# Dummy products on TensorE ahead of a group norm's variance and between the steps of a token router

## The chip, the cores and the metric

The kernel runs on one NeuronCore of a Trainium2 chip. The metric is the device time of one execution in microseconds (us). Five engines work side by side, each on its own list of instructions: TensorE (PE in the profile, its weight loads PEld), VectorE (DVE), ScalarE (ACT), GpSimd (POOL) and SyncE (SP), which issues the transfers. They wait for each other through semaphores that the kernel sets by hand. TensorE's clock has two levels, 1.2 and 2.4 GHz; the profile shows the granted clock as a share of the upper one, so 0.50 is 1.2 GHz and 1.00 is 2.4 GHz.

## The reference

Two transformer-like layers with adaptive layer norms, each an attention-like part and a feed-forward part. The input has 2048 tokens of 128 features. The change touches the first layer only, in two places. Cut to these:

```python
# layer 0, attention part (16 heads of 8 features, scan over 2048 tokens)
S = dt[..., None] * S + kv ; o = einsum('bhk,bhkv->bhv', rt, S_old + u * kv)
mean = jnp.mean(o, axis=-1, keepdims=True)          # group norm over each head
var = jnp.var(o, axis=-1, keepdims=True)
o = (o - mean) * jax.lax.rsqrt(var + EPS_GN) * gn_w + gn_b
x = x + (o * g).reshape(B, T, D) @ Wo
...
# layer 0, feed-forward part: each token goes to one of 8 experts, 128 places each
routes = softmax(x @ w_switch + b_switch).argmax(-1)
oh = (routes[:, None] == jnp.arange(E)[None, :]).astype(jnp.int32)
pos = (jnp.cumsum(oh, axis=0) * oh).sum(-1) - 1
keep = pos < capacity
slot = jnp.where(keep, routes * capacity + pos, E * capacity)
buf = zeros.at[slot].set(x)                          # dispatch
```

The second layer (a Mamba-like scan over 16 states and a mixture of 16 experts plus a shared one) follows and takes the time from about 240 us to the end.

## The kernel before, in words

Features or head values lie on the 128 partitions, the 2048 tokens along the free dimension, in 4 chunks of 512. One chunk is one PSUM bank of TensorE's output. `sequences()` (L166) lists, by engine, every step in the order in which that engine does it; `upto(step, i)` turns a step into the semaphore value to wait for, `done(step, i)` into the increment at its end. Each engine works its list strictly in that order, so an instruction whose data are ready still stands behind the one before it.

**The group norm.** After the scan, each chunk i goes through: `gn_centred` on TensorE (L728, subtracts the head's mean by a matrix product), `gn_sq` on ScalarE (L1148, a square; the helper's line also serves other squares), `gn_var` on TensorE (L733, the mean of squares, into PSUM bank `VAR_BANK[i]`), then on ScalarE `gn_ln` (L1248), `gn_rs` (L1250) and `gn_rs2` (L1252). ScalarE takes chunk i to its end before it squares chunk i+1. So its list is a chain that goes to TensorE and back once a chunk. VectorE scales and normalizes (L1670, L1676, L1678), GpSimd multiplies by the gate (L2008), TensorE multiplies by `Wo` (L739, L743). TensorE's order around the change comes from `TAIL_PE` (L154): at turn 33 of the loop at L753 it does four `reduce` products (L776), `gn_centred(1)`, `gn_var(0)`, `gn_var(1)`, `gn_centred(2)`; then come the last `reduce` products, `gn_var(2)`, `gn_centred(3)` and so on (L780 to L794). Chunk 0's `gn_centred` was done two turns earlier, and its square is made while TensorE does the reduces.

**The router.** On TensorE: `varD` (L812), 16 small products for the logits (`router`, L840, recorded as two each), 8 transposes of the layer's input (`h_turn`, L845), a wait for VectorE's one-hot matrix (`r_oh`), the products `prefix` and `totals` (L850, L851), 8 more transposes, a wait for VectorE's kept slots (`r_kept`), a transpose of the slots (`slot_turn`, L855) and then 16 times `dispatch(t)` (L864), four products of 512 columns each. VectorE (L1736 for all its router steps) goes from the logits to `r_oh`, then `r_shift`, `r_base`, a rounding remainder (L1754), and, once `totals` is there, `r_cum` to `r_kept`. Then it makes `onehot(t)` (L1784) in two buffers: `onehot(t)` waits for `dispatch(t - 2)`, `dispatch(t)` for `onehot(t)`.

The constants that the change uses are `EYEB` (128x128, bf16) and `sel` (96 x 32 x 128, bf16). They are loaded at the start (L631, L632) and counted by `wc_loaded`.

Of the kernel before, what the change touches and what calls it, by code (L numbers as in the profile page):

```python
# [152 lines left out]
VAR_BANK = (2, 0, 3, 1)  # L153
# [212 lines left out]
def build(nc, X_in, vec_in, core_in, cst_in, wA_in, wmod_in, cstB_in, wB1_in, wB2_in, wC_in, sel_in, eyeb_in, wD_in, out):  # L366
# [17 lines left out]
    with ctx:  # L384
        def sb(name, shape, dt=f32):
            return ctx.enter_context(nc.sbuf_tensor(name, shape, dt))

        def sem(name):
            return ctx.enter_context(nc.semaphore(name))

        vec_loaded, core_loaded, wmod_loaded, cst_loaded, wa_loaded, cstb_loaded, wb_loaded, wc_loaded, out_stored = map(
            sem, ["vec_loaded", "core_loaded", "wmod_loaded", "cst_loaded", "wa_loaded", "cstb_loaded", "wb_loaded", "wc_loaded", "out_stored"])
# [11 lines left out]
        def upto(step, i=0):  # L404

            engine, n = count[step, i]
            return finished[engine], n

        def done(step, i=0):

            engine, n = count[step, i]
            assert order[engine].pop(0) == (step, i), (step, i)
            return finished[engine], 1
# [5 lines left out]
        def column(step, q):  # L419

            return upto(step.format(ORDER[q % DK]), q // DK)
# [15 lines left out]
        sel = sb("sel", [96, 2 * NS, P], bf16)  # L437
        BC = sb("bc", [96, T], bf16)
        EYEB = sb("eyeb", [P, P], bf16)
# [20 lines left out]
        def CORE_(name):  # L460
            a, w = core_at[name]
            return core[:, a:a + w]

        def C(name, part=slice(None)):
            a, w = cst_at[name]
            return cst[part, a:a + w]
# [5 lines left out]
        def CB_(name):  # L472
            a, w = cb_at[name]
            return cstB[:, a:a + w]
# [121 lines left out]
        def ch(buf, i, off=0):  # L596

            return buf[:, i * N + off:(i + 1) * N + off]

        def half(h, i, rows=P):  # L600

            return ps[0:rows, (4 * h + i) * N:(4 * h + i + 1) * N]

        def bank(b, lo=0, hi=P):
            return ps[lo:hi, b * N:(b + 1) * N]
# [72 lines left out]
        def _(pe):  # L678
            mm = nc.tensor.matmul
# [36 lines left out]
            def gate_and_bonus(i):  # L716
# [5 lines left out]
                pe.wait_ge(*(upto("bonus", i - 1) if i else upto("w_exp", 1)))  # L722
                mm(bank(1), C("head_sum"), ch(M2, i), start=True, stop=True).then_inc(*done("head_ruk", i))

            def gn_centred(i):
                pe.wait_ge(*upto("o", i))
                pe.wait_ge(*column("scan{}", NR - NCH + i))
                mm(half(1, i), C("gn_centre"), ch(O, i), start=True, stop=True).then_inc(*done("gn_centred", i))  # L728

            def gn_var(i):  # L730
                pe.wait_ge(*upto("gn_sq", i))
                pe.wait_ge(*(column("scan{}", (2 * DK - 1) if i == 0 else NR - 1) if i % 2 == 0 else upto("o", LAST - 1 + i // 2)))
                mm(bank(VAR_BANK[i]), C("gn_mean"), ch(T1, i), start=True, stop=True).then_inc(*done("gn_var", i))  # L733
# [11 lines left out]
            def ms_c(i):  # L745
                pe.wait_ge(*upto("sqC", i))
                pe.wait_ge(*upto("gn_norm", i))
                mm(bank(VAR_BANK[i]), CORE_("mean"), ch(T2, i), start=True, stop=True).then_inc(*done("msC", i))

            tail = {"gn_centred": gn_centred, "gn_var": gn_var}  # L750
            lora_b(0)
            pe.wait_ge(*upto("spread_r"))
            for q in range(NR + LAG_R - 1):  # L753
                i, v = q // DK, ORDER[q % DK]
# [12 lines left out]
                if q >= LAG_R and (q - LAG_R) % 4 == 0:  # L767

                    pe.wait_ge(*column("prod{}", q - LAG_R + 3))
                    for r in range(q - LAG_R, q - LAG_R + 4):  # L770
                        i, v = r // DK, ORDER[r % DK]
# [5 lines left out]
                for name, i in TAIL_PE.get(q, ()):  # L777
                    tail[name](i)

            gn_var(2)  # L780
            gn_centred(3)
            wo_b(0)
            gn_var(3)
            wo(0)
            wo_b(1)
# [58 lines left out]
            def h_turn(t):  # L844
                nc.tensor.transpose(ps[:, 4 * N + t * P:4 * N + (t + 1) * P], HB[:, t * P:(t + 1) * P], CORE_("eye")).then_inc(*done("h_turn", t))  # L845

            for t in range(NT // 2):
                h_turn(t)
            pe.wait_ge(*upto("r_oh"))
            mm(bank(1)[:, 0:P], CB_("tri"), small(3), start=True, stop=True).then_inc(*done("prefix"))  # L850
            mm(bank(2)[:, 0:P].rearrange("p (e t) -> p e t", e=E0), CB_("ones"), small3(3).rearrange("p t e -> p e t"), start=True, stop=True).then_inc(*done("totals"))  # L851
            for t in range(NT // 2, NT):
                h_turn(t)
            pe.wait_ge(*upto("r_kept"))
            nc.tensor.transpose(bank(1, 0, NT)[:, 2 * P:3 * P], tiny(9), CORE_("eye")).then_inc(*done("slot_turn"))  # L855
            for t in range(NT):
                if t == SCALE_AT:
                    pe.wait_ge(*upto("r_scale"))
                    nc.tensor.transpose(bank(2, 0, NT)[:, 2 * P:3 * P], tiny(4), CORE_("eye")).then_inc(*done("scale_turn"))
                pe.wait_ge(*upto("onehot", t))  # L860
                pe.wait_ge(*upto("h_turned_lo", t // 4))
                for part in range(2):
                    for j in range(2):
                        last = mm(bank(3 * j), HT[:, part, t * P:(t + 1) * P], OH1[:, t % 2, j * N:(j + 1) * N],  # L864
                                  start=(t == 0 and part == 0), stop=(t == NT - 1 and part == 1))
                last.then_inc(*done("dispatch", t))
# [242 lines left out]
            for q in range(NQ):  # L1109
                i, n = divmod(q, NS)  # L1110
# [1127 lines left out]
```

## Time and profile before

| | us |
|---|---|
| three runs | 658.53, 660.23, 660.22 (median 660.22) |
| the profiled execution, its own time | 658.89 |
| its span, first to last instruction | 657.1 |
| TensorE busy | 564.2 (86%) |
| VectorE busy | 530.9 (81%) |
| ScalarE busy | 392.1 (60%) |
| GpSimd busy | 394.3 (60%) |
| mean granted clock of TensorE | 0.953 |

The three runs and the profiled one lie at two levels 1.7 us apart. What lies outside the span is 658.89 - 657.1 = 1.8 us. Busy shares are means over stages that differ: the two places of the change lie at 103 to 118 us and at 160 to 191 us of the span. In a timeline row a group of like instructions is merged: the first number is its start, the second the time that it covers, xN how many there are, and the bracket says how long the engine stood idle before it and what released it. A 128x512 product on fp32 data is recorded as two.

### The profile page before, as it was taken

How to read it: one execution, taken by the hardware profiler on the slowest of the kernel's cores; microseconds unless marked ns; L12 is line 12 of the kernel's file. 1: busy time of each engine (PE TensorE's matmuls, PEld its weight loads, DVE VectorE, ACT ScalarE, POOL GpSimd, SP SyncE). 2: the span in 40 equal slices, each digit the busy share in tenths (PEclk: the TensorE clock that was granted, in tenths of full speed). 3: DMA queues.
4: the chain of work that ended last, by engine and by line, in shares of the span. 5: the costliest groups of instructions: out<-in, count | busy, mean ns of one | idle time of the engine just before them, and what ended most of it. 6: DMA issues, size and time to landing. Idle time of an engine off the chain costs nothing.

```text
span 657.1 us, 6791 instructions
## 1 busy us (share of the span) xinstructions
PE 564.2 (86%) x1896; PEld 316.2 (48%) x1896; DVE 530.9 (81%) x727; ACT 392.1 (60%) x672; POOL 394.3 (60%) x345
## 2 busy tenths in 40 slices
PE   6698668899899868688888768878879999999997
PEld 3233222366678523233333323323336768888885
DVE  1979997656779676699999999999998857666664
ACT  5675324686123497777966756766565475555553
POOL 0035886651000201389999999999976546566665
PEclk9798878999699999699999899999999999999999
DMA  8100000700110001000001000000103334434330
GB/s 309 37 1 0 0 1 9 332 1 1 65 65 0 1 0 48 1 0 0 0 5 44 24 25 24 24 14 7 43 0 104 107 105 123 129 111 145 109 102 17
DMA packets 14598, 35.13 MB, mean 53 GB/s; under 512 B 1952, under 2 KB 2240, under 8 KB 13952
## 3 DMA queue, kind: packets, MB, share of 16 engines
q1 hardware_dynamic: 14560, 34.69, 16.5%
q8 instruction: 16, 0.26, 0.2%
q14 instruction: 22, 0.18, 0.1%
HBM read 33.48 MB, written 1.20 MB: 53 GB/s over the span
## 4 chain that ended last, share of the span: by engine, by line
DVE 19%; PE 14%; issue 13%; POOL 10%; ACT 3%; POOLq 0%; DVEq 0%; ACTq 0%
DVE arena L1928 13%; POOL h_parts L2144 9%; PE ps L1079 7%; DVE arena L1903 5%; PE ps L1014 4%; POOL arena L2008 1%; PE ps L1117 1%; PE ps L942 1%; PE ps L1051 0%; ACT ps L1488 0%; ACT arena L1477 0%; PE ps L1026 0%; ACT L1435 0%; ACT arena L1437 0%; DVE arena L1912 0%
## 5 line engine op out<-in xcount | busy, mean ns | idle before, releaser
L2008 POOL TENSOR_TENSOR arena<-arena 128x512 f32<-128x512 f32 x184 | 226.0, 1256 | 24.0 <-DVE arena L1928 19.1
L1928 DVE TENSOR_TENSOR_SCAN arena<-ps,carry,arena 128x512 f32<-128x512 f32 x128 | 156.5, 1265 | 0.0
L1014 PE MATMUL ps<-arena,core 128*128 128x512 f32 x256 | 126.7, 613 | 1.3 <-POOL arena L2008 0.8
L1488 ACT ACTIVATE ps<-arena,abase 128x512 f32<-128x512 f32 x128 | 88.0, 691 | 63.9 <-DVE arena L1928 63.0
L2144 POOL TENSOR_TENSOR h_parts<-arena,h_parts 128x512 fp32r<-128x512 f32 x68 | 87.8, 1291 | 62.1 <-ACT h_parts L1528 61.1
L1079 PE MATMUL ps<-x_parts,w_hi 128*128 128x512 f32 x272 | 100.4, 408 | 0.4 <-DVE arena L2001 0.4
L1903 DVE TENSOR_TENSOR arena<-ps,arena 128x1024 f32<-128x1024 f32 x64 | 76.9, 1202 | 5.8 <-PE ps L1117 5.8
L1996 DVE TENSOR_TENSOR ps<-ps,arena 128x512 f32<-128x512 f32 x64 | 44.6, 698 | 43.0 <-PE ps L1079 36.7
L1117 PE MATMUL ps<-bc,sel 96*128 96x512 bf16 x128 | 44.2, 393 | 40.7 <-ACT arena L1477 23.8
L1536 ACT ACTIVATE arena<-ps 128x512 f32<-128x512 f32 x68 | 40.6, 599 | 61.3 <-PE ps L1079 60.2
L1014 PEld LDWEIGHTS ps<-arena,core 128*128 128x128 f32 x256 | 48.5, 194 | 42.2 <-issue 22.4
L1079 PEld LDWEIGHTS ps<-x_parts,w_hi 128*128 128x128 f32 x272 | 51.2, 188 | 14.6 <-issue 1.4
L1117 PEld LDWEIGHTS ps<-bc,sel 96*128 96x128 bf16 x128 | 12.2, 98 | 92.6 <-ACT arena L1477 37.8
L1079 PE MATMUL ps<-x_parts,wD 128*128 128x512 f32 x136 | 54.0, 397 | 0.0
L1079 PE MATMUL ps<-h_parts,w_hi 128*128 128x512 f32 x136 | 53.4, 396 | 0.3 <-POOL h_parts L2144 0.3
L2059 POOL TENSOR_TENSOR x<-arena,x 128x512 f32<-128x512 f32 x4 | 5.3, 1320 | 71.6 <-DVE arena L1829 71.6
L2001 DVE TENSOR_TENSOR arena<-ps,arena 128x512 f32<-128x512 f32 x64 | 44.2, 691 | 2.2
L1528 ACT ACTIVATE h_parts<-arena 128x512 fp32r<-128x512 f32 x68 | 42.4, 623 | 4.8 <-DVE arena L2001 4.2
L1477 ACT ACTIVATE arena<-ps 128x512 f32<-128x512 f32 x64 | 37.3, 583 | 1.0 <-PE ps L1117 0.7
L761 PE MATMUL ps<-v_parts,spread_r 128*128 128x512 f32 x64 | 26.7, 521 | 11.9 <-DVE arena L1661 11.9
L2012 POOL TENSOR_TENSOR v_parts<-arena,v_parts 128x512 fp32r<-128x512 f32 x4 | 6.3, 1613 | 41.1 <-ACT v_parts L1202 41.1
L1661 DVE TENSOR_TENSOR_SCAN arena<-arena,ps 128x512 f32<-128x512 f32 x24 | 29.7, 1262 | 0.0
(256 smaller groups left out, 1003.4 us busy)
## 6 DMA issues: line engine op xcount, KB each, us to landing
arena<-weight_rows SPq DMA_DIRECT2D x64, 256.0 KB, 3.3
arena<-in_wB SPq DMA_DIRECT2D x2, 2048.0 KB, 12.6
arena<-in_wD SPq DMA_DIRECT2D x8, 384.0 KB, 3.1
arena<-in_cstB SPq DMA_DIRECT2D x1, 1368.0 KB, 5.9
wC<-in_wC SPq DMA_DIRECT2D x1, 1056.0 KB, 11.7
x<-in_x SPq DMA_DIRECT2D x4, 256.0 KB, 4.6
arena<-slot_rows SPq DMA_DIRECT2D x4, 256.0 KB, 3.6
arena<-scale_rows SPq DMA_DIRECT2D x4, 256.0 KB, 3.6
```

The lines of the kernel that those rows point to most:

```text
L1014: mm(bank(c + 2 * (i % 2)), CORE_("eye"), PRC[:, (2 * q + c) % PR_RING, :], start=False, stop=(n == NS - 1)).then_inc(*done(f"y{n}_{c}", i))
L1079: r = mm(out, w_parts[wp][:, k, :], x[xp], start=start and (wp, xp) == (0, 0), stop=stop and last)
L1117: mm(bank(b), sel[:, row, :], BC[:, i * N:(i + 1) * N], start=True, stop=True).then_inc(*done(f"{kind}{n}", i))
L1488: A(bank(6 + c), ch(DTG[:, c, :], i), ACT.Exp, scale=ABASE[:, c * NS + n:c * NS + n + 1]).then_inc(*done(f"dec{n}_{c}", i))
L1528: A(HWP[:, 0, q % 4, :], (HW if e < E1 else HH)[:, q % H_RING, :], ACT.Copy).then_inc(*done(f"h_hi{e}", i))
L1536: A(SG[:, q % 2, :], bank(4 + q % 2), ACT.Silu).then_inc(*done(f"silu{e}", i))
L1903: tt(DBU[:, a:a + DI, :], bank(4).unsqueeze(1).to_broadcast([P, DI, N]), DU[:, :, i * N:(i + 1) * N], ALU.mult).then_inc(*done(f"dbu{n}", i))
L1928: nc.vector.tensor_tensor_scan(ST[:, k % ST_RING, :], bank(6 + c), DBU[:, (2 * q + c) % DBU_RING, :], CARRY[:, k:k + 1], ALU.mult, ALU.add ...
L1996: tt(bank(6 + k) if e < E1 else HH[:, h, :], bank(6 + k), SG[:, k, :], ALU.mult).then_inc(*done(f"hh{e}", i))
L2001: tt(HW[:, h, :], bank(6 + k), ROW[r % W_SLOTS], ALU.mult).then_inc(*done(f"hw{e}", i))
L2008: mul = lambda o, a, b: nc.gpsimd.tensor_tensor(o, a, b, ALU.mult)
L2144: nc.gpsimd.tensor_tensor(HWP[:, 1, q % 4, :], (HW if e < E1 else HH)[:, q % H_RING, :], HWP[:, 0, q % 4, :].bitcast(f32), ALU.subtract).t ...
```

## The change

A helper `keep_busy(b, n)` issues n products of the constants `EYEB` and `sel` (96 rows, 128 columns of weights, 512 moving columns, bf16) into PSUM bank b. Nothing reads them and they increment no semaphore. Ten stand ahead of the waits of `gn_var(0)`, with a wait for the constants' loads; five ahead of the wait for `r_oh`, eight ahead of the wait for `r_kept`, and two between `slot_turn` and the first `dispatch`.

```diff
@@ -722,12 +722,20 @@
+            def keep_busy(b, n):
+
+                for _ in range(n):
+                    mm(bank(b), EYEB[0:96, :], sel[:, 0:4, :], start=True, stop=True)
+
...
             def gn_var(i):
+                if i == 0:
+                    pe.wait_ge(wc_loaded, 48)
+                    keep_busy(VAR_BANK[0], 10)
                 pe.wait_ge(*upto("gn_sq", i))
...
@@ -846,13 +854,16 @@
             for t in range(NT // 2):
                 h_turn(t)
+            keep_busy(3, 5)
             pe.wait_ge(*upto("r_oh"))
             mm(bank(1)[:, 0:P], CB_("tri"), small(3), ...).then_inc(*done("prefix"))
             mm(bank(2)[:, 0:P]..., CB_("ones"), ...).then_inc(*done("totals"))
             for t in range(NT // 2, NT):
                 h_turn(t)
+            keep_busy(3, 8)
             pe.wait_ge(*upto("r_kept"))
             nc.tensor.transpose(bank(1, 0, NT)[:, 2 * P:3 * P], tiny(9), CORE_("eye")).then_inc(*done("slot_turn"))
+            keep_busy(3, 2)
             for t in range(NT):
```

## Rows read from the trace of the kernel before

**Rows 1.** Windows: us, then each engine's busy time, granted clock (PEclk), DMA; group norm.

```profile
core 0: us, PE busy (x) PEld busy (x) DVE busy (x) ACT busy (x) POOL busy (x), PEclk, DMA share, GB/s
104.50:108.00 3.50, 1.15 (x3) 0.19 (x1) 2.63 (x4) 2.25 (x4) 3.50 (x4) 1.00 0.00 0
108.20:111.40 3.20, 3.16 (x4) 1.17 (x4) 0.92 (x2) 1.02 (x2) 1.27 (x2) 0.50 0.00 0
```

**Rows 2.** Windows, the router and the dispatch.

```profile
160.90:165.10 4.20, 3.81 (x33) 3.62 (x32) 2.44 (x4) 1.88 (x4) 0.00 (x0) 1.00 0.00 0
166.20:169.40 3.20, 2.07 (x9) 2.04 (x10) 2.72 (x9) 0.98 (x3) 0.00 (x0) 0.50 0.00 0
173.00:176.20 3.20, 3.20 (x9) 2.52 (x8) 1.70 (x3) 0.00 (x0) 0.00 (x0) 0.50 0.63 213
176.50:180.00 3.50, 3.25 (x14) 2.00 (x13) 3.26 (x8) 0.00 (x0) 0.00 (x0) 1.00 0.24 81
```

**Rows 3.** Timeline of TensorE, group norm: start, us, engine, line, op.

```profile
103.67 1.13 PE L728 MATMUL ps<-arena 128*128 128x512 f32 x2
104.63 1.02 PE L733 MATMUL ps<-arena 128*128 128x512 f32 x2
108.24 2.07 PE L733 MATMUL ps<-arena 128*128 128x512 f32 x2 [2.59 <-ACT arena L1148]
...
112.90 1.12 PE L733 MATMUL ps<-arena 128*128 128x512 f32 x2
```

**Rows 4.** Timeline of ScalarE, group norm.

```profile
102.78 0.60 ACT L1148 ACTIVATE arena<-ps 128x512 f32<-128x512 f32 x1 [0.46 <-PE ps L728]
105.69 0.69 ACT L1248 ACTIVATE arena<-ps,vec 128x512 f32<-128x512 f32 x1 [2.31 <-PE ps L733]
...
107.60 0.58 ACT L1148 ACTIVATE arena<-ps 128x512 f32<-128x512 f32 x1
110.35 0.69 ACT L1248 ACTIVATE arena<-ps,vec 128x512 f32<-128x512 f32 x1 [2.16 <-PE ps L733]
...
114.06 0.69 ACT L1248 ACTIVATE arena<-ps,vec 128x512 f32<-128x512 f32 x1 [1.22 <-PE ps L733]
```

**Rows 5.** Timeline of TensorE, two bf16 products in a row at full clock.

```profile
295.84 0.60 PE L1117 MATMUL ps<-bc,sel 96*128 96x512 bf16 x2
296.28 1.02 PE L1014 MATMUL ps<-arena,core 128*128 128x512 f32 x2
```

**Rows 6.** Timeline of TensorE, the router.

```profile
165.12 1.07 PE L845 MATMUL ps<-core,arena 128*128 128x128 f32 x8
167.33 0.79 PE L850 MATMUL ps<-arena 128*128 128x128 f32 x2 [1.14 <-DVE arena L1736]
...
168.39 1.89 PE L845 MATMUL ps<-core,arena 128*128 128x128 f32 x8
170.63 0.38 PE L855 MATMUL ps<-core,arena 128*16 128x128 f32 x1 [0.35 <-DVE arena L1736]
171.42 8.26 PE L864 MATMUL ps<-onehot,h_turned 128*128 128x512 f32 x24 [0.41 <-DVE onehot L1784]
```

**Rows 7.** Timeline of VectorE, the router and the dispatch.

```profile
168.68 0.42 DVE L1736 TENSOR_TENSOR_SCAN arena<-arena,ps 128x128 f32<-128x128 f32 x1 [0.27 <-PE ps L851]
...
170.61 1.42 DVE L1784 TENSOR_SCALAR onehot<-arena 128x1024 fp32r<-128x1024 f32 x2
...
173.53 0.75 DVE L1784 TENSOR_SCALAR onehot<-arena 128x1024 fp32r<-128x1024 f32 x1 [0.91 <-PE ps L864]
175.24 0.75 DVE L1784 TENSOR_SCALAR onehot<-arena 128x1024 fp32r<-128x1024 f32 x1 [0.95 <-PE ps L864]
...
186.43 0.75 DVE L1784 TENSOR_SCALAR onehot<-arena 128x1024 fp32r<-128x1024 f32 x1 [0.29 <-PE ps L864]
...
188.47 0.75 DVE L1784 TENSOR_SCALAR onehot<-arena 128x1024 fp32r<-128x1024 f32 x1 [0.31 <-PE ps L864]
```

**Rows 8.** Timeline, the end of the dispatch and ScalarE's copy that waits for it.

```profile
190.50 0.60 ACT L1320 ACTIVATE arena<-ps 128x512 f32<-128x512 f32 x1 [4.74 <-PE ps L864]
```

## The prediction

> **What bounds the kernel now.** I read the windows with the granted clock first, since the change adds work that nothing uses and can pay only through the clock of TensorE. The clock is at 2.4 GHz up to 108.0 us, at 1.2 GHz from 108.2 to 111.4 us [rows 1], and again at 1.2 GHz from 166.2 to 176.2 us [rows 2]. Both falls come behind little streaming on TensorE: 2.59 us of idleness before the second variance product [rows 3], and the logits' products from 160.9 to 165.1 us [rows 2], whose moving operand has 8 columns. Then I read the timelines around the two places. In the group norm the chain is ScalarE's: its logarithm of chunk 0 begins at 105.69 us, that of chunk 1 at 110.35, that of chunk 2 at 114.06 [rows 4], so a round takes 4.66 us with the variance product at half clock (2.07 us) and 3.71 us with it at full clock (1.12 us) [rows 3]. In the router the chain is VectorE's, with TensorE's `prefix` and `totals` in between, and from 171.42 us on it is the dispatch on TensorE and the one-hots on VectorE, which release each other [rows 6, 7]. All that follows hangs on the end of the dispatch at 190.50 us [rows 8].
>
> **The price of one dummy product.** Two bf16 products of the same size take from 295.84 to 296.28 us, so 0.22 us each at full clock [rows 5]. At half clock a product costs twice that: an fp32 variance product goes from 1.12 to 2.07 us [rows 3], and four dispatch products at half clock set a pace of 175.24 - 173.53 = 1.71 us, 0.43 each [rows 7]. I take 0.22 and 0.43 us.
>
> **Ten products ahead of gn_var(0).** The square that `gn_var(0)` waits for begins at 102.78 us and takes 0.60, so it is ready at 103.38 [rows 4], before `gn_centred(1)` begins at 103.67. `gn_var(0)` begins at 104.63, right behind the 1.13 us of `gn_centred(1)`, with no idle time in its row [rows 3]. There is no wait here to fill. The ten products go between the two and push `gn_var(0)` back by 10 x 0.22 = 2.2 us, and with it ScalarE's logarithm at 105.69, which had waited 2.31 us for just this product [rows 4]. The rest of the chain starts from there, so 2.2 us are on the path; the added wait for the loads is free, since they are over long before.
>
> What comes back is the half clock of `gn_var(1)`, at most 4.66 - 3.71 = 0.95 us. But the idle stretch of 2.59 us lies between `gn_var(0)` and `gn_var(1)` [rows 3], that is behind the new products, and it stays as long as it was: logarithm, exponential, square, square on ScalarE. The products only move it later. So the clock may fall all the same and catch `gn_centred(2)` or `gn_var(2)`. Bounds: 2.2 - 0.95 = 1.25 us where the fall is avoided, 2.2 + 0.95 = 3.15 us where a second product is caught as well. I take half of the 0.95 as won: **+1.7 us**.
>
> The Trainium skill (TensorE: Matmul & The Clock Gate, on why this matters for kernels) asks for a TensorE kept busy without gaps between bursts. By it the ten products would be a gain where they bridged a gap; the row shows none ahead of `gn_var(0)`, so the sum above goes by the row.
>
> **Five products ahead of r_oh.** TensorE is idle for 1.14 us before `prefix` at 167.33 [rows 6]. Five products last 1.1 us at full clock and 2.15 at half. The fall at 166.2 us follows from the logits' products before it, which the change leaves as they are, so I take half clock: `prefix`, `totals` and all of VectorE's steps behind them (`totals` releases the scan at 168.68 [rows 7]) come 2.15 - 1.14 = 1.0 us later. Bounds: 0 and 1.0.
>
> **Eight products ahead of r_kept and two behind slot_turn.** Before, the second transposes last from 168.39 to 170.28 us, then there are 0.35 us of idleness, the slots' transpose at 170.63, and the first dispatch at 171.42 [rows 6]. What decides is when the clock is back. From 108.2 us steady work brought it back after some 3.3 us [rows 1]. In the router it took until between 176.2 and 176.5 us, since there the work had holes until the dispatch began at 171.42 [rows 2, 6]. The dummy products close the holes, so from 166.2 us on TensorE is all but busy.
> - Clock back near 169.5 us: by then five products, `prefix` and `totals` are done; eight transposes at full clock 1.1 us (1.07 at 165.12 [rows 6]), eight products 1.8, `slot_turn` 0.3, two products 0.4: the dispatch begins near 173.1 us. At full clock two turns take 188.47 - 186.43 = 2.04 us [rows 7], so 1.02 to 1.07 each with VectorE's side work, 16 turns about 17.1: it ends at 190.2 against 190.5 [rows 8], -0.3 us.
> - Clock back near 172.9 us: transposes 1.9, most of the eight products at 0.43; the dispatch begins near 174.4 and ends at 191.5, +1.0 us.
> - Bounds: the clock never at half: dispatch from 171.5, all 16 turns at full clock, end at 188.6, -1.9 us. Clock back no sooner than before: 1.0 + 8 x 0.43 + 2 x 0.43 = 5.3 us less the idle 0.35 and 0.4 that they fill, so a start at 175.9, and an end near 193.0, +2.5 us.
>
> I take **+0.2 us**, between the first two and nearer to the first. The loads of the slots' rows and the scale's rows move with `slot_turn` and stay hidden by the experts' work; no queue but TensorE's has anything put ahead. PSUM banks 2 and 3 are free there, so nothing else waits for the dummies.
>
> **Sum.** 1.7 + 0.2 = +1.9 us. Against the profiled execution, 658.89, that makes 660.8. The median of the three runs, 660.22, is 1.3 above it; the four times of before lie at two levels and have a mean of 659.5, so I add the sum to that: **661.4 us**, 0.2% over the median. About 0.3% (2.0 us: 658.2 to 662.2) is what a measurement can tell from no change, and the forecast lies inside, near its upper end.
>
> **The rivals.**
> - *The routing's dummies run at half clock throughout (slower).* Eight products stand before a wait of 0.35 us; at half clock they are 3.4 us ahead of `slot_turn` and thereby of every dispatch. The point that decides is whether the clock is back before they begin. For it: nothing in the change touches the products that made it fall, and it stayed low through `prefix`, `totals` and transposes before [rows 2, 6]. Against it: the holes are closed. 659.5 + 1.7 + 2.5 = 663.7 us. Chance 0.27.
> - *The clock is held at both places.* 1.25 - 1.9 = -0.65 us, 658.9 us. For it: the group norm's clock was up for all of `gn_var(0)`. Against it: the logits. Chance 0.15. The Trainium skill's rule cited above, taken for the whole change, comes to this case.
> - *The ten products cost nothing.* That needs a wait ahead of `gn_var(0)` that the row of the trace hides, or slack in ScalarE's chain: then -0.95 - 1.9 = -2.85, 656.7 us. Against it: rows 3 and 4 show neither. Chance 0.08.
> - *The forecast.* Chance 0.50. Its own range is 659.9 to 662.9: group norm 1.25 to 2.2, router -0.3 to +1.0, and half a microsecond for the level on which the runs fall.
>
> **How the numbers follow.** Faster by over 0.3% (below 658.2): the third rival 0.08 and the lower part of the second 0.04, so 0.12. Slower by over 0.3% (above 662.2): the first rival 0.25, the upper part of the forecast 0.18, so 0.43. Within: 0.45. The range for 8 in 10 takes in the forecast, most of the first rival and most of the second: 658.7 to 663.9 us.
>
> **What would show it.** In the changed kernel's timeline ten rows of bf16 products between the second L728 and the first variance product, that product about 2.2 us later, and ScalarE's wait for it 4.5 instead of 2.3 us. The idle time between the first and the second variance product near 2.6 us again. In the windows, a half clock that still begins between 163 and 168 us but ends before 173. The first dispatch between 172.5 and 174.5 us, taken without the shift of the group norm, and one-hots at a pace of 1.0 us from the first. The forecast is wrong if the first variance product does not move, or if TensorE's idleness behind it is gone; wrong for the router if the granted clock there is 1.00 throughout, or 0.50 during most of the dispatch.

## The result and the profile after

The changed kernel takes 663.75 us (median of 6 runs, 662.0 to 664.63) against 659.94 us before (6 runs, 658.53 to 660.31): a ratio of 1.0061 with an interval of 1.0046 to 1.0075, slower by 3.8 us. The forecast was 661.4 us, a loss of 1.2 us against the median. The profiled execution took 663.61 us with a span of 661.7, so 4.6 us more than the 657.1 of before.

I followed the extra time along the kernel by putting the same instruction of both traces side by side:

| instruction | before, us | after, us | delay |
|---|---|---|---|
| logarithm of chunk 0 (L1248, after L1259) | 105.69 | 107.79 | +2.1 |
| logarithm of chunk 1 | 110.35 | 111.53 | +1.2 |
| logarithm of chunk 2 | 114.06 | 116.05 | +2.0 |
| logarithm of chunk 3 | 117.77 | 119.76 | +2.0 |
| first router step of VectorE | 165.37 | 168.14 | +2.8 |
| router's scan, released by `totals` | 168.68 | 172.95 | +4.3 |
| VectorE's copy at the end of the dispatch | 190.50 | 192.82 | +2.3 |
| `bc_r1` of the second layer, its last of four (L1837, after L1848) | 263.13 | 266.08 | +2.9 |
| last of the state's expansion (L1903) | 494.51 | 497.89 | +3.4 |
| first product of the last experts (L1996) | 502.05 | 506.76 | +4.7 |

So three parts make the 4.6 us: the group norm 2.0, the router 0.3, and 2.3 behind the dispatch, where no line of the kernel was changed.

**Group norm.** TensorE's timeline of the changed kernel, the rows that answer to [rows 3] (L728 is now the line of the dummies, L733 `gn_centred`, L741 `gn_var`, L784 the `reduce` products):

```profile
103.60 1.12 PE L733 MATMUL ps<-arena 128*128 128x512 f32 x2
104.57 2.32 PE L728 MATMUL ps<-sel,eyeb 96*128 96x512 bf16 x10
106.73 1.02 PE L741 MATMUL ps<-arena 128*128 128x512 f32 x2
110.33 1.16 PE L741 MATMUL ps<-arena 128*128 128x512 f32 x2 [2.59 <-ACT arena L1159]
111.30 1.91 PE L733 MATMUL ps<-arena 128*128 128x512 f32 x2
113.13 1.82 PE L784 MATMUL ps<-arena 128*32 128x512 f32 x8
```

The ten dummies fill 106.73 - 104.57 = 2.16 us and move the first variance product by the same amount (104.63 to 106.73 us). The idle time behind it is 2.59 us, to the hundredth what it was. ScalarE's wait for that product, 2.31 us in [rows 4], is longer by the dummies:

```profile
107.79 0.69 ACT L1259 ACTIVATE arena<-ps,vec 128x512 f32<-128x512 f32 x1 [4.47 <-PE ps L741]
...
111.53 0.69 ACT L1259 ACTIVATE arena<-ps,vec 128x512 f32<-128x512 f32 x1 [1.25 <-PE ps L741]
...
116.05 0.69 ACT L1259 ACTIVATE arena<-ps,vec 128x512 f32<-128x512 f32 x1 [2.02 <-PE ps L741]
```

The windows of the same stretch, columns as in [rows 1]:

```profile
104.50:107.70 3.20, 3.20 (x13) 1.26 (x11) 1.63 (x2) 0.00 (x0) 3.20 (x3) 1.00 0.00 0
107.80:111.20 3.40, 0.86 (x2) 0.49 (x3) 2.00 (x3) 2.42 (x4) 0.00 (x0) 1.00 0.00 0
111.40:114.60 3.20, 3.20 (x11) 0.43 (x9) 0.69 (x1) 2.43 (x4) 1.20 (x1) 0.50 0.00 0
```

The clock falls all the same, at 111.3 instead of 108.1 us. The second variance product is now at full clock (1.16 instead of 2.07 us), which wins back 0.9 us at chunk 1; but `gn_centred(2)` (1.91 us, before 1.71) and the `reduce` products (1.82 us, before 1.06) are caught, and at chunk 2 the delay is 2.0 us again.

**Router.** TensorE's timeline, the rows that answer to [rows 6] (L848 the logits, L853 transposes, L859 and L860 `prefix` and `totals`, L865 `slot_turn`, L875 `dispatch`):

```profile
166.16 1.88 PE L848 MATMUL ps<-arena 128*128 128x8 f32 x8 [0.18 <-DVE arena L1567]
167.89 1.95 PE L853 MATMUL ps<-core,arena 128*128 128x128 f32 x8
169.63 2.34 PE L728 MATMUL ps<-sel,eyeb 96*128 96x512 bf16 x5
171.76 0.64 PE L859 MATMUL ps<-arena 128*128 128x128 f32 x2
172.19 0.66 PE L860 MATMUL ps<-arena 128*128 128x128 f32 x2
172.67 1.06 PE L853 MATMUL ps<-core,arena 128*128 128x128 f32 x8
173.56 1.89 PE L728 MATMUL ps<-sel,eyeb 96*128 96x512 bf16 x8
175.29 0.27 PE L865 MATMUL ps<-core,arena 128*16 128x128 f32 x1
175.40 0.59 PE L728 MATMUL ps<-sel,eyeb 96*128 96x512 bf16 x2
175.69 6.25 PE L875 MATMUL ps<-onehot,h_turned 128*128 128x512 f32 x24
```

```profile
166.00:172.60 6.60, 6.44 (x25) 5.19 (x26) 2.90 (x10) 1.45 (x3) 0.00 (x0) 0.50 0.01 2
...
172.90:178.00 5.10, 5.10 (x28) 3.32 (x27) 4.62 (x11) 1.35 (x3) 0.00 (x0) 1.00 0.01 2
```

The clock fell at about the same time of the record as before (165.9), but the work is 2 us later, so the last logits and the first transposes are caught too (1.88 instead of 1.06 us, and 1.95 instead of 1.07). The five dummies take 2.13 us at half clock and hold `prefix` back; that is the +4.3 us at the scan. Then the clock is back after 6.8 instead of 10.2 us, the whole dispatch runs at full clock, and 2 us come back by its end. As much comes back in e1 below, without any of the router's dummies.

**Behind the dispatch.** Two stretches at half clock are new or longer. These are windows of the kernel before, at the entry to the last experts:

```profile
490.50:493.70 3.20, 3.20 (x8) 1.66 (x8) 3.20 (x4) 1.90 (x3) 3.20 (x4) 0.50 0.00 0
494.00:497.00 3.00, 3.00 (x13) 1.75 (x13) 2.64 (x4) 1.25 (x3) 1.88 (x3) 1.00 0.00 0
```

and of the changed one, at the same work:

```profile
493.70:497.00 3.30, 3.30 (x10) 1.97 (x9) 3.30 (x4) 1.90 (x3) 3.30 (x4) 0.50 0.00 0
497.10:500.30 3.20, 3.20 (x7) 1.61 (x7) 2.50 (x4) 1.29 (x2) 1.81 (x3) 0.50 0.00 0
```

TensorE is the bound there (fully busy), and four products that took 1.88 us at full clock take 3.05 (the first row is of before, the second of the changed kernel):

```profile
494.52 1.88 PE L1014 MATMUL ps<-arena,core 128*128 128x512 f32 x4
498.07 3.05 PE L1025 MATMUL ps<-arena,core 128*128 128x512 f32 x4
```

With their neighbours that makes +1.3 us between the last two lines of the table. The other is a stretch from 261.6 to 264.8 us. Before, the same work was at full clock:

```profile
258.30:265.00 6.70, 3.83 (x10) 1.78 (x11) 3.34 (x7) 6.56 (x10) 4.02 (x4) 1.00 0.35 117
```

In the changed kernel the delay is 2.0 us ahead of this stretch (0.4 us had come back near 248 us) and 3.0 us behind it:

```profile
261.60:264.80 3.20, 3.20 (x5) 1.13 (x5) 0.22 (x1) 2.93 (x4) 1.88 (x2) 0.50 0.61 229
265.00:268.20 3.20, 2.12 (x7) 0.95 (x6) 2.06 (x3) 2.67 (x5) 2.28 (x3) 1.00 0.00 0
268.40:278.40 10.00, 5.85 (x9) 2.24 (x10) 6.20 (x6) 8.13 (x13) 2.50 (x3) 0.50 0.00 1
```

### The profile page after: what moved, and what is told of

It is laid out like the page before. It is cut to its first block, busy times and chain, and to the rows that moved or that the text cites. A ratio compares the mean times of both kernels' runs of the same rounds, so it can differ in the third digit from the quotient of the medians.

```text
span 661.7 us, 6841 instructions
## 1 busy us (share of the span) xinstructions
PE 572.1 (86%) x1921; PEld 319.2 (48%) x1921; DVE 530.8 (80%) x727; ACT 392.2 (59%) x672; POOL 394.1 (60%) x345
## 4 chain that ended last, share of the span: by engine, by line
PE 16%; DVE 15%; issue 13%; POOL 13%; ACT 3%; POOLq 0%; DVEq 0%; ACTq 0%
DVE arena L1939 10%; POOL h_parts L2155 9%; PE ps L1090 7%; PE ps L1025 5%; DVE arena L1914 4%; POOL arena L2019 4%; PE ps L1128 1%; PE ps L953 1%; PE ps L1062 1%; ACT ps L1499 1%; ACT arena L1488 0%; PE ps L1016 0%; ACT L1446 0%; PE ps L1055 0%; PE ps L1037 0%
## 5 line engine op out<-in xcount | busy, mean ns | idle before, releaser
L1025 PE MATMUL ps<-arena,core 128*128 128x512 f32 x256 | 128.5, 622 | 1.1 <-POOL arena L2019 0.7
L953 PE MATMUL ps<-arena,wC 128*128 128x512 f32 (+1 forms) x48 | 27.7, 708 | 2.7 <-ACT arena L1388 2.7
```

The costliest lines, as they stand in the source:

```text
L1025: mm(bank(c + 2 * (i % 2)), CORE_("eye"), PRC[:, (2 * q + c) % PR_RING, :], start=False, stop=(n == NS - 1)).then_inc(*done(f"y{n}_{c}", i))
```

## The experiments

**Theory.** The group norm's dummies stand where TensorE did not wait and are paid in full; the router's are near neutral; the rest is not work of the dummies, but the delay, which moves the second layer against the moments at which the clock falls. **Rivals:** the router's dummies are the main cost; the dummies themselves cost something in the second layer; a part of them is hidden.

The 16 profiles differ by up to 2.6 us before 40 us already, whatever the kernel. Seven of them (e1, e4, e6, e8, e9, e12, e14) have a half-clock stretch that begins at 17 to 18 us, which the other nine lack, and they reach the group norm 1.2 us or more later than any of the nine. So every delay of the profiles in the table is counted from one and the same scan of VectorE ahead of the group norm (before: 104.37 us, the seven 106.0 to 106.4, the nine 103.8 to 104.8), against the profile of before. "Dispatch" is VectorE's copy at its end, "last" one of its last instructions (654 us). Each ratio is to the runs of before that were taken beside that kernel. The edits of e1, e2, e8, e10 and e12 are shown against the changed kernel, those of e3, e4, e7 and e9 against the kernel before, where the helper `keep_busy` is added and not shown.

| profile of | chunk 0's logarithm | chunk 3's | dispatch | last | median of the runs | ratio to before, interval |
|---|---|---|---|---|---|---|
| the change | +2.2 | +2.1 | +2.4 | +4.7 | 663.75 | 1.0061, 1.0046 to 1.0075 |
| e1, group norm's ten alone | +2.2 | +2.1 | +0.9 | +0.4 | 659.81 | 1.0011, 0.9984 to 1.0037 |
| e2, router's alone | 0.0 | 0.0 | -1.2 | +0.4 | 660.31 | 1.0012, 0.9992 to 1.0033 |
| e3, nine in the wait | 0.0 | -0.9 | -2.2 | -3.3 | 658.42 | 0.9979, 0.9951 to 1.0006 |
| e4, ten copies on ScalarE | +1.0 | +1.8 | +0.5 | -0.3 | 660.67 | 1.0008, 0.9989 to 1.0026 |
| e5, the change again | +2.2 | +2.0 | +2.4 | +4.6 | 663.91 | 1.0056, 1.0037 to 1.0074 |
| e6, before again | 0.0 | 0.0 | 0.0 | +1.6 | 660.48 | 1.0011, 0.9991 to 1.0031 |
| e7, twenty at the group norm | +4.3 | +3.4 | +3.3 | +3.2 | 663.02 | 1.0047, 1.0032 to 1.0062 |
| e8, nine in the wait and the router's | 0.0 | -0.9 | -0.7 | -0.2 | 659.28 | 0.9998, 0.9984 to 1.0012 |
| e9, eleven behind the dispatch | 0.0 | 0.0 | 0.0, then +2.3 | +4.6 | 665.28 | 1.0081, 1.0064 to 1.0097 |
| e10, the change and four there | +2.2 | +2.1 | +2.4, then +3.2 | +2.9 | 663.97 | 1.0057, 1.0037 to 1.0077 |
| e11, e3 again | 0.0 | -0.9 | -2.2 | -3.3 | 659.74 | 0.9994, 0.9976 to 1.0012 |
| e12, ten, and five in the router | +2.2 | +2.1 | +3.9 | +3.4 | 663.75 | 1.0061, 1.0037 to 1.0085 |
| e13, e10 again | +2.2 | +2.1 | +2.4, then +3.2 | +2.8 | 664.76 | 1.0067, 1.0042 to 1.0091 |
| e14, e3 a third time | 0.0 | -0.9 | -2.2 | +0.9 | 661.88, one run | |

### e1, the group norm's ten dummies alone

```diff
-            keep_busy(3, 5)
...
-            keep_busy(3, 8)
...
-            keep_busy(3, 2)
```

> The ten dummies at the group norm alone, none in the router. Theory (they stand where TensorE did not wait, and push ScalarE's chain): the first variance product 2.1 to 2.2 us later, the logarithm of chunk 3 about 2.0 us later than before, and that delay still there at the end of the dispatch; time over before by 2 us, plus or minus what the half-clock stretches of the second layer take elsewhere (up to 2 us). Rival (the router's dummies are the main cost): under 0.7 us over before.

The group norm came as expected, 2.2 and then 2.1 us. But at the end of the dispatch only 0.9 us of it were left and at the end 0.4: the router without dummies lay better against the clock than in the profile of before (6.8 us at half clock instead of 10.2), and won 1.2 us. With the router's dummies added, which is the changed kernel, the dispatch ends at +2.4: in the change's own setting they cost 1.5 us. The median says no difference. So the group norm's 2.1 us are real, and they do not alone make the change's 3.8.

### e2, the router's dummies alone

```diff
                 if i == 0:
                     pe.wait_ge(wc_loaded, 48)
-                    keep_busy(VAR_BANK[0], 10)
```

> The router's 5, 8 and 2 dummies alone. Theory: the end of the dispatch moves by between -0.3 and +1.0 us; time within 1 us of before, apart from later half-clock stretches. Rival (the router's dummies are the main cost): 3 us or more over before, with the dispatch ending 2.5 us or more later.

The dispatch ended 1.2 us earlier, more than the theory gave: the clock was low for 3.4 us only, back near 169.8 us, and the five dummies moved the scan by 0.5 us. The time is that of before. The rival, that they are the main cost, falls. Neither half of the change costs by itself what the two cost together.

### e3, e11, e14, nine dummies in the wait

```diff
             def gn_var(i):
+                if i == 1:
+                    pe.wait_ge(wc_loaded, 48)
+                    pe.wait_ge(*upto("o", LAST - 1))
+                    keep_busy(VAR_BANK[1], 9)
                 pe.wait_ge(*upto("gn_sq", i))
```

> Nine dummies in the wait behind the first variance product, ahead of the second, none elsewhere. Theory (the number was right, the place wrong): they fit in the 2.59 us of idleness, the second variance product keeps the full clock, 1.1 instead of 2.1 us, and the logarithm of chunk 3 comes 0.95 us EARLIER than before; time 0.5 to 1.5 us under before. Rival (the clock falls whatever is put there): no change of that product, 0 to +0.3 us.

> The nine dummies behind the first variance product again, more runs. Theory: the logarithm of chunk 3 is 0.95 us earlier than in the kernel before, counted from the scan in front; the median lies 1 to 2 us under before. Rival (its first runs were luck): a median within 0.5 us of before.

> The nine dummies in the wait once more, one look. Both its profiles were of executions near 656 us, while most runs lay near 659.7. If an execution near 660 is caught, its group norm is 0.95 us earlier as in the two others and the 3.5 us are lost elsewhere, in half-clock stretches of the router or the second layer that the other two did not have.

TensorE's timeline of e3 (L742 is `gn_var`):

```profile
104.99 1.02 PE L742 MATMUL ps<-arena 128*128 128x512 f32 x2
106.70 2.10 PE L728 MATMUL ps<-sel,eyeb 96*128 96x512 bf16 x9 [0.69 <-DVE arena L1658]
108.64 1.08 PE L742 MATMUL ps<-arena 128*128 128x512 f32 x2
```

The added wait for `o` is one that `gn_var(1)` has itself, taken ahead of the dummies. The nine fit into the wait, the second variance product keeps the full clock, and chunk 3 is 0.9 us earlier in all three profiles. That is the gain that the change was after, and it needs the other side of `gn_var(0)`. On the whole kernel it does not show reliably: in 23 runs the times go from 655.4 to 662.5 us, seven of them under 657.5 and ten within 1 us of 660, and the second median is within 0.6 us of that of before beside it. Still, none of the 90 runs of before that stand beside the result and the experiments lies under 657.7 us. So in some executions the gain is there, 2.8 to 2.9 us between the profiled ones that start as early (656.02 and 656.12 against 658.89 of before), and how large it is on the average stays open. The third profile, 661.88 us, has the same group norm and the same early dispatch, but loses 3.1 us behind it (-2.2 to +0.9), in longer half-clock stretches, where the other two won 1.1. My expectation of 1 to 2 us did not hold in e11.

### e4, the delay without dummies

```diff
                 act.wait_ge(*upto("gn_var", i))
+                for k in range(10 if i == 0 else 0):
+                    A(ABASE[:, k:k + 1], vec[:, k:k + 1], ACT.Copy)
```

> No dummy at all; instead ten small copies on ScalarE, about 2 us together, between the first variance product and its logarithm, which only delay the same chain. Theory (the 2.3 us that the changed kernel loses behind the router come from the mere delay, which moves the work against the moments at which the clock falls): a time over before by about as much as with the ten dummies alone, plus 1.0 us (the clock falls at 108 us as before or one round later), and falls in the second layer at other places than before. Rival (the dummies themselves cost in the second layer): over before by exactly the delay of the group norm, nothing more behind it.

The ten copies took 1.0 instead of 2 us, so the delay was too small for what it was to show. It grew to 1.8 us at chunk 3, since the clock, low for the second variance product as before, was still low for the `reduce` products ahead of the third (1.87 us, before 1.06), and nothing of it was left at the end. Inconclusive for the theory; e9 is the better form of it.

### e5 and e6, both kernels again

> The changed kernel once more, for a second profile in which the clock falls at other moments of the work, and for more runs. If the 2.3 us that it lost behind the dispatch belong to the moments at which the clock fell in that execution, this profile loses another amount there (between -1.5 and +1.5 us against before), the group norm again 2.0 us and the router between -0.5 and +1.5; the runs spread over 3 us or more. If they belong to the dummies, the loss behind the dispatch is again 2.0 to 2.5 us and the median again 3.8 us over before.

> The kernel before once more, for a second profile. If the clock's falls come at moments of their own, in this profile at least one of the half-clock stretches in the group norm (3.4 us) or the router (10.2 us) starts elsewhere or lasts another time, and the router's part, from the logarithm of chunk 3 to the end of the dispatch, is up to 1.3 us shorter, as it was in the three kernels of the first experiments whose router had no dummies. If they are tied to the work, all stretches lie where they lay.

In both, what I had taken for the sign of falls at moments of their own did not come. The changed kernel's second profile loses 2.2 us behind the dispatch again, and its median is again 3.8 us over that of before (663.91 against 660.14, ratio 1.0056). The kernel before, in its second profile, has the group norm and the router as in the first, but enters the last experts 1.7 us later: there, too, the clock was low for twice as long, in a kernel without one dummy.

```profile
492.60:495.80 3.20, 3.20 (x9) 1.71 (x7) 3.20 (x4) 1.90 (x3) 3.20 (x4) 0.50 0.00 0
496.00:499.20 3.20, 3.20 (x8) 1.78 (x8) 2.41 (x3) 1.29 (x2) 1.90 (x3) 0.50 0.00 0
```

So the doubled stretch at the last experts does not need a delay; the stretch at 261.6 us is in neither profile of before. But the falls are not at random against the work either. Counted from the scan, the half-clock stretch that begins at 26.2 us before begins within 0.6 us in all 16 profiles, and a given delay met the same falls behind it in both profiles of the change.

### e7, twenty at the group norm, none in the router

```diff
             def gn_var(i):
+                if i == 0:
+                    pe.wait_ge(wc_loaded, 48)
+                    keep_busy(VAR_BANK[0], 20)
                 pe.wait_ge(*upto("gn_sq", i))
```

> Twenty instead of ten dummies ahead of the first variance product, none in the router. Theory (each stands on the path with its full length): the logarithm of chunk 0 comes 20 x 0.216 = 4.3 us later than in the kernel before, counted from the scan in front of it, twice the 2.17 us of ten; chunk 3's 3.4 to 4.3 us later; median 2 us over that of the ten alone. Rival (a part of them hides in a wait): under 4.0 us at chunk 0.

```profile
104.53 4.48 PE L728 MATMUL ps<-sel,eyeb 96*128 96x512 bf16 x20
108.85 1.02 PE L741 MATMUL ps<-arena 128*128 128x512 f32 x2
112.45 1.12 PE L741 MATMUL ps<-arena 128*128 128x512 f32 x2 [2.58 <-ACT arena L1156]
113.42 1.02 PE L733 MATMUL ps<-arena 128*128 128x512 f32 x2
```

4.32 us for twenty, twice the 2.16 of ten: each is on the path in full. The idle time behind is 2.58 us once more, this time without a fall. And from chunk 1 on the delay stays 3.2 to 3.4 us to the end, where ten dummies and those of the router had grown from 2.4 to 4.7. With 663.02 us it is as slow as the change within the intervals, from another sum.

### e8, nine in the wait and the router's as in the change

```diff
                 if i == 0:
                     pe.wait_ge(wc_loaded, 48)
-                    keep_busy(VAR_BANK[0], 10)
+                if i == 1:
+                    pe.wait_ge(wc_loaded, 48)
+                    pe.wait_ge(*upto("o", LAST - 1))
+                    keep_busy(VAR_BANK[1], 9)
```

> Nine dummies behind the first variance product, where TensorE waits, and the router's 5, 8 and 2 as in the change. If only the place at the group norm was wrong, this one runs under before by 0.5 to 2.5 us. If the router's dummies cost on the average, it runs over the nine alone by 0.5 us or more.

The same time as before (0.9984 to 1.0012), where the changed kernel, which differs from it in the group norm's dummies alone, is 3.8 us slower. By its own expectation it settles nothing more: it does not run clearly under before, and its median, 659.28 us, lies between those of e3 and e11 (658.42 and 659.74). Against e3 the router's dummies cost 1.5 us at the end of the dispatch (-0.7 instead of -2.2).

### e9, the delay by another way

```diff
             pe.wait_ge(*upto("h_turned_lo", NCH - 1))
+            pe.wait_ge(wc_loaded, 48)
+            keep_busy(6, 11)
             e_up(0)
```

> The kernel before with eleven dummies behind the end of the dispatch, on TensorE right ahead of the experts' first products (L873), and none elsewhere. They push all that follows by 11 x 0.216 = 2.4 us, as the change did by another way. Theory (a push of 2.4 us moves the second layer against the clock's falls and costs 2.3 us more): delay 2.4 us at the experts, 4.3 to 5.0 us at the end, median 4 to 5 us over before. Rival (the loss in the second layer comes from the changed group norm or router): 2.4 us at the end.

```profile
193.28 2.53 PE L728 MATMUL ps<-sel,eyeb 96*128 96x512 bf16 x11 [0.83 <-ACT arena L1327]
195.65 1.95 PE L878 MATMUL ps<-arena 128*128 128x128 f32 x16
```

This is the deciding one. Group norm and router are those of before, the eleven dummies take 2.37 us and delay the experts by 2.3, and the kernel ends 4.6 us later, by 2.3 us more, as in the changed kernel. The extra comes in the same two places: 1.0 us by the work that stood at 263 us before, and 1.4 us at the entry to the last experts:

```profile
263.80:267.00 3.20, 3.20 (x5) 1.07 (x4) 0.00 (x0) 2.68 (x4) 2.13 (x2) 0.50 0.55 214
...
495.90:499.10 3.20, 3.20 (x10) 2.02 (x9) 3.20 (x3) 1.89 (x3) 3.20 (x4) 0.50 0.00 0
499.30:502.50 3.20, 3.20 (x6) 1.48 (x7) 2.58 (x4) 1.39 (x3) 1.84 (x4) 0.50 0.00 0
```

The second of these places has its doubled stretch in e6 as well, so one profile cannot put it down to the delay: against e6 the end is 3.0 us later and not 4.6. What carries the conclusion is the times: the median is 6.1 us over before, and the lower end of the interval, 1.0064, is 4.2 us, from four runs. So a delay of 2.3 us costs clearly more than itself; nothing of the changed group norm or router is needed. The delay is made of dummies here too; that it is not they that cost is said by e7, where twenty of them cost nothing behind the dispatch.

### e10 and e13, the change with more delay

```diff
             pe.wait_ge(*upto("h_turned_lo", NCH - 1))
+            keep_busy(6, 4)
             e_up(0)
```

> The changed kernel with four more dummies ahead of the experts' first products, 0.86 us more delay, 3.2 us in all at that place; twenty dummies at the group norm had come to 3.2 us there and lost nothing behind it. Theory: MORE dummies, yet 1 to 1.5 us FASTER than the changed kernel at the end, the delay of 3.2 us staying 3.1. Rival (every dummy adds, nothing depends on where the falls lie): 0.86 us slower than the changed kernel, 5.5 us over before.

> The changed kernel with four more dummies at the experts once more. Its first profile ended 1.8 us before the changed kernel's (counted from the same scan), yet three of its four runs lay at 664. If the profile was one of two patterns of the clock's falls, a profile or runs near 664 go with a half-clock stretch of 6.8 us instead of 3.4 near 493 us or a third one before 270 us, and the runs split into a group near 661 and one near 664. If four more dummies are simply no gain, nearly all runs lie at 664 or over.

In both profiles more work ends sooner: from 3.2 us of delay behind the dispatch to 2.9 at the end, 1.8 us under the change. But of the eleven runs of the two only the two profiled ones, 661.28 and 661.56, are of this kind; the others lie at 663.5 to 665.2, and the medians are not below the change's. Both profiled ones are of the nine that reach the scan early. So the profiles bear out that the loss depends on where the delay puts the work; that four more dummies would be a gain is not so in most executions, and what those look like no profile here shows.

### e12, without the eight and the two

```diff
             keep_busy(3, 5)
...
-            keep_busy(3, 8)
...
-            keep_busy(3, 2)
```

> The change without the eight and the two dummies; ten at the group norm and five ahead of the one-hot's wait stay. If the five alone make the loss in the router: prefix 1.5 us later against the logits, as in the changed kernel, and the end of the dispatch within 0.3 us of where the changed kernel has it, 2.4 us after before. If the eight and two make it: the dispatch ends 0.7 us or more earlier than in the changed kernel.

Neither of the two. The dispatch ends 1.5 us LATER than with all of them:

```profile
171.37 2.34 PE L728 MATMUL ps<-sel,eyeb 96*128 96x512 bf16 x5
173.50 0.63 PE L859 MATMUL ps<-arena 128*128 128x128 f32 x2
...
176.63 0.28 PE L864 MATMUL ps<-core,arena 128*16 128x128 f32 x1 [1.18 <-DVE arena L1745]
177.42 5.03 PE L873 MATMUL ps<-onehot,h_turned 128*128 128x512 f32 x13 [0.51 <-DVE onehot L1793]
```

```profile
174.20:177.50 3.30, 1.61 (x12) 1.12 (x11) 2.60 (x8) 1.35 (x3) 0.00 (x0) 1.00 0.00 0
177.70:181.00 3.30, 3.30 (x9) 2.56 (x9) 1.68 (x3) 0.00 (x0) 0.00 (x0) 0.50 0.32 83
```

The clock had come back, TensorE was idle for 1.18 and 0.51 us, and the clock fell again just as the dispatch began. So the eight and two do what they are for: in the changed kernel they hold the clock into the dispatch. Without all three groups (e1) the clock, back at 174.8 us, stayed up as well. The five ahead of them are what costs in the router, by holding `prefix` back 1.5 us, in both kernels. The delay of 3.9 us at the end of the dispatch is 3.4 at the end: as in e7, a longer delay than the change's did not grow. The median is that of the change all the same, 663.75 us.

## Why the prediction was wrong

**The group norm: right, and short by 0.4 us.** "There is no wait here to fill" held; the ten cost 2.16 us against 2.2. The idle stretch stayed at 2.59 us and the fall moved one round on. Of the 0.95 us at stake I took half as won; the measured gain is 0.1 us (a delay of 2.2 us at chunk 0 and of 2.1 at chunk 3), for the fall cost 0.8 us again at chunk 2. The term was +1.7, measured +2.0 to +2.1.

**The router: right in the sum (+0.2 against +0.3), by luck.** The sum was made against a router that stood where it stood before. With the group norm's ten alone (e1) the router wins 1.2 us without one dummy, and the dummies then cost 1.5 us; where nothing shifts it (e2) they win 1.2 us. +0.3 is what is left of two moves that the prediction did not have. The prices along the way added up otherwise too: the logits at half clock +0.8 us, which I had not counted; the five dummies 1.5 us at `prefix` and not 1.0, for TensorE reached them late; then the dispatch all at full clock. The clock was back at 172.7 us, 170.7 without the group norm's shift, between my two cases. The rival that they all run at half clock did not come about: its price, +2.5 us, is not in the trace, and that its total of 663.7 us is nearly the measured one is chance. So is it that 663.75 us lies inside the range for 8 in 10, whose upper end was there for this rival. I had put the fall near 166 us down to the logits' products. In all 16 profiles it comes between 2.4 us before and 1.0 us after the end of these products, but no run changed them, so this cause is not shown.

**Behind the dispatch: this is the step that failed.** The sum ended with the dispatch, on the tacit claim that a delay there is a delay of the same size at the end ("all that follows hangs on the end of the dispatch"). Between the profiles it grew from 2.4 to 4.7 us. e9 shows that 2.3 us of delay with the old group norm and router does the same (in the times it costs more, 4.2 us at the lower end of the interval), e7 that 3.3 us of delay does not, and e6 that the longer half clock at the last experts comes in the kernel before as well. The profile of before showed the second layer's half-clock stretches, and I had called the price of one in the group norm 0.95 us, but gave the move of the later ones no term and no place in the range beyond half a microsecond. Every sign that I had named for the stages of the change came: the first variance product 2.1 us later, ScalarE's wait 4.47 us, the half clock from 165.9 to 172.7 us, the first dispatch at 175.69 us, 173.7 without the group norm's shift. No sign looked behind the dispatch.

**The size.** Between the two profiled executions the time grew by 4.7 us and the sum said 1.9. Of the 2.8 us that it lacked, 2.3 are those behind the dispatch and 0.5 those of the group norm and the router. The medians lie 3.8 us apart and not 4.7, since the median of before is 1.0 us over its profiled execution. So by the medians the part behind the dispatch is nearer to 1.4 us (3.8 - 2.4) than to 2.3. My base, the mean of four times, 659.5, was a little low: the 90 runs of before have a median of 659.8. And the forecast's own range was added up wrongly: 659.5 + 2.2 + 1.0 + 0.5 is 663.2, not 662.9, and it took 2.2 us for the group norm where its bound had been 3.15.

In e3 nine dummies in a wait of TensorE hold the clock (1.08 instead of 2.07 us for the product behind them), and in e12, without the eight and the two, it falls behind 1.18 and 0.51 us of idleness. The Trainium skill's advice to keep TensorE busy (TensorE: Matmul & The Clock Gate, "Why this matters for your kernels") agrees with both.

**What stays open.** Why e1 and e2 cost nothing in the median, where their sum costs 3.8 us, is explained by the profiles only for the profiled executions: with either half alone the delays behind the dispatch are others. The profiles show two differences between executions that come in the kernel before as well: the later start, 2.0 us at the scan between e6 and the first profile, and the doubled stretch at the last experts, 1.7 us there; what else makes the runs of one kernel spread by 3 to 7 us is not known, for there are one to three profiles of each.

## What to carry to other kernels

Before filling a wait with dummy products, look for the wait in the row of the very instruction that they go ahead of: here the row of `gn_var(1)` had 2.59 us of idleness in its bracket and that of `gn_var(0)` none, and the same dummies cost 2.1 us at one place and won 0.9 us at the other. Judge such a change by where the granted clock falls in the whole kernel, not in the stage that was changed: between two profiles a delay of 2.4 us grew to 4.7 us in stages that TensorE bounds, and a longer one of 3.3 us did not grow. And a gain of a microsecond in one stage of a kernel whose clock falls a dozen times needs many runs; here 23 runs of a clean local gain of 0.9 us did not settle its size.

## What the runs showed of the hardware

- The clock fell after the same idle stretch of 2.6 us in some kernels and not in others: at 108.1 us before, one round later in the changed kernel, not at all in this stage with twenty dummies, whose idle stretch was 2.58 us. What counts is more than the length of the idle time.
- Eight products with 32 weight columns took 1.06 us at full clock, and 1.82 us when the clock was low for most of them.
- Products of 512 bf16 columns follow each other at 2.16 us / 10 = 0.22 us at full clock and 2.13 us / 5 = 0.43 us at half.
- Ten copies of one column on ScalarE took 1.0 us together, 0.1 us each.
